# A four-layer graph network on one core: unread matmuls in TensorE's pauses, group 1's set-up products moved, and the last group's order rewritten

## The chip, the cores and the metric

One core of one Trainium2 chip runs the whole program as one launch. Its engines run side by side and wait for each other only through semaphores: TensorE (PE), VectorE (DVE), ScalarE (ACT), GpSimd (POOL) and SyncE (SP), which here only starts DMAs. The metric is the device time of one execution in microseconds (us).

## The reference, cut to what matters

A batch of 16 graphs, each of 512 nodes by 128 features, goes through four layers. Each is `x = layernorm(x + layer(x, adj))` over the features, in fp32.

```
x: (16, 512, 128), adj: (512, 512)
layer 0: concat([x, x*s, x*s*s, ...]) @ W + b      # s: sums over rows or columns of adj and of an adaptive softmax matrix
layer 1: batchnorm(relu(batchnorm((A_hat @ x) @ W1.T + b1)) @ W2.T + b2)   # statistics over all 16*512 rows
layer 2: twice relu(adj @ (h @ Wg + bg)); then for p = 1..4 an LSTM over windows of p nodes, whose last state
         replaces the last node of each window
layer 3: h = x @ fc.T + fcb; eight times h = h + 1/8 * (alph*0.5*(adj @ h - h) + h @ w_eff - h + x)
```

The eight Euler steps of layer 3 are linear in `h` and `x`. The kernel computes them as a polynomial in the matrix of the steps: x3 (the layer's input), two multiplications by powers of the matrix (`power1`, `power2`), combinations with precomputed coefficient matrices `e` (`coefs`), and two more multiplications by its cube, which a Horner scheme needs (`inner`, then `giant`). A constant row, `euler_bias`, stands for what `fcb` adds over the eight steps.

## The kernel before, in words

`D` is 128 features, `N` 512 nodes, in `NT` = 4 tiles of 128. A product that must be exact to fp32 is three matmuls of rounded parts (high x high, high x low, low x high; `matmul3`, lines 136 to 138), so an input of TensorE is first written as a high part (a cast, mostly on ACT) and a low part (the difference, on DVE or POOL). A PSUM bank holds 128 x 512 fp32.

The program has two halves.

The first half does layer 0 and layer 1 for all 16 batches. `phase_a` runs over slots q = 0..9 with a pair of batches in each: `products` (layer 0, ended on DVE), `aggregate` (A_hat times x, slot q-1, 24 matmuls of 128x512 for the pair) and `hidden` (times W1, slot q-2). Slot 0 has no aggregate yet and slot 8 no products. After it comes `second` (line 777), which waits for the batch norm over all rows and multiplies by W2 for each batch, each in two fp32 matmuls of 128x512. Then the block ends, with a barrier of all engines.

The second half works in groups of two batches, g = 0..7. The loop for group g does, on every engine, four things at once: the LSTMs of group g (layer 2) in eleven cells c0..c10; layer 3 of group g-1 (`L3_NAMES`); the `giant` products, their sum and the last norm of group g-2 (`DONE_NAMES`); the graph convolution of group g+1 (`FRONT_NAMES`). The order is written out by hand in tables, one list of names per engine and cell: an engine runs its part of cell c and then the names in list c. A cell's chain is: gate matmuls on TensorE, ACT (sigmoids and tanh), DVE (state), ACT, DVE (state and next input, high and low, `in_h`, `in_l`), and TensorE again. Between a cell's matmuls TensorE runs the names, and they are what fills the time the chain takes. For example, and only of TensorE:

```python
FILL_PE = [[], ["giant_2", "giant_3", "giant_0", "giant_1", "turn_0"], ["x3t_0", "power1a_0"],
           ["power1b_0", "power2_0", "gather0_0"], ["coefs0_0", "weight0_0"], ...
TAIL_PE = [["giant_2", "giant_3", "giant_0", "giant_1", "x3t_0", "x3t_1", "power1a_0", ...
LATE_PE, ... = ({1: ["lift_last", "bias"]}, ...      # added to FILL_PE's lists in group 1
```

Tables `START_*` and `ONCE_*` stand for the time before group 0 and for group 0; `FILL_*` with the `LATE_*` names for group 1; `FILL_*` for groups 2 to 6; `LAST_*` for group 7; `TAIL_*` has two lists behind it, layer 3 of group 7 with the `giant`s of group 6, and the `giant`s of group 7. What stands in the tail has no LSTM beside it.

Group 0 also computes constants of layer 3: the matrix powers, `lift` and `lift_last` (24 matmuls in all, the bias row's vectors lifted by the cube), `turn_vec`, `bias` (line 1921: the row times ones, into a bank, copied by DVE to `euler_bias`, semaphore `bias_kept`), and `split_e`, the low part of `e`.

`x3sum` takes the norm's statistics on DVE (line 1434); POOL turns them into mean and variance (lines 1179 to 1186) and into rstd and shift (line 1187, a power, and 1188), `root`; ACT applies them (line 1276), casts the high part (line 1313); POOL makes the low part (line 1206). `x3t` (line 1760) transposes the result; `power1a` and `power1b` are its product with the matrix, by halves of the tiles. `hturn` (line 1820) turns the LSTM's state back, `x3add` adds it to the layer's input.

## Time and profile before

| | us |
|---|---|
| median of 3 runs | 998.44 (998.06 to 1000.43) |
| the profiled execution, its own time | 999.66 |
| its span, first to last instruction | 997.7 |
| TensorE busy | 912.7 (91%) |
| VectorE busy | 648.7 (65%) |
| ScalarE busy | 578.3 (58%) |
| GpSimd busy | 309.7 (31%) |
| mean granted TensorE clock | 0.957 of full speed |

Busy times come from one profiled execution. A matmul's duration overlaps its neighbours' in the trace: what one costs in a dense stretch is the distance from its start to the next one's start. The granted clock has two levels, full speed (2.4 GHz) and half (1.2 GHz); a value between them for a stretch is a mean.

### The profile page before, as it was taken

Reading aid. Unit: us, or ns where it says so; the run is one execution under the profiler, and the core shown is the slowest. Engines: PE = TensorE matmul, PEld = TensorE weight load, DVE = VectorE, ACT = ScalarE, POOL = GpSimd, SP = SyncE. Lnnn points to the kernel's source line nnn. Section 1 sums busy time; section 2 is a strip of 40 time slices with the busy share of each in tenths; the row PEclk is TensorE's granted clock in tenths of the full one; section 3 lists DMA queues with packets and bytes.
Section 4 is the critical chain, followed back from the end, with each engine's and each line's share of the span. In section 5 each row is a group of like instructions: output and inputs, shape, how many; then the busy total and the mean of one; then the engine's idle time right before and its main releaser. Section 6 shows DMA issues by size and latency. Waiting matters only on the chain.

```text
span 997.7 us, 14843 instructions
## 1 busy us (share of the span) xinstructions
PE 912.7 (91%) x5034; PEld 790.2 (79%) x5034; DVE 648.7 (65%) x1554; ACT 578.3 (58%) x1292; POOL 309.7 (31%) x555
## 2 busy tenths in 40 slices
PE   6799996957999799999999999999999999999695
PEld 4688884446888479988998998898899899888584
DVE  6689994766577665576667667666666765755522
ACT  5366755742564457467657746755774684575331
POOL 3666551032210322144126215303521620230412
PEclk9799997978999989999999999999999999999897
DMA  5322101310100110101201010110110001001000
GB/s 174 117 75 64 68 28 42 148 55 9 32 1 12 42 33 11 43 1 43 64 1 43 28 38 11 33 64 1 43 64 1 12 22 33 1 11 33 1 22 22
DMA packets 26595, 38.55 MB, mean 39 GB/s; under 512 B 3333, under 2 KB 12422, under 8 KB 26010
## 3 DMA queue, kind: packets, MB, share of 16 engines
q1 hardware_dynamic: 26088, 36.05, 10.8%
q10 hardware_dynamic: 434, 1.57, 0.5%
q8 instruction: 40, 0.66, 0.3%
q14 instruction: 33, 0.27, 0.1%
HBM read 21.89 MB, written 15.73 MB: 38 GB/s over the span
## 4 chain that ended last, share of the span: by engine, by line
PE 57%; POOL 7%; DVE 7%; ACT 5%; issue 2%; ACTq 0%; DMA 0%; SPq 0%; POOLq 0%; DVEq 0%
PE psum L136 16%; PE psum L138 16%; PE psum L137 16%; PE psum L1707 2%; PE psum L1708 2%; PE psum L1711 2%; POOL x_rstd L1187 1%; ACT x L1276 1%; POOL out_rstd L1187 1%; ACT raw L1341 1%; POOL node_l L1197 1%; ACT gate L1245 1%; DVE x_stats L1434 1%; DVE nat_l L1579 1%; DVE tl L1482 1%
## 5 line engine op out<-in xcount | busy, mean ns | idle before, releaser
L1245 ACT ACTIVATE gate<-psum,gate_bias 128x256 f32<-128x256 f32 (+2 forms) x296 | 144.4, 559 | 88.0 <-PE psum L1711 70.2
L136 PE MATMUL psum<-in_h,wih_h 128*128 128x256 f32 (+2 forms) x312 | 108.0, 346 | 8.7 <-DVE in_l L1428 6.4
L137 PE MATMUL psum<-in_l,wih_h 128*128 128x256 f32 (+2 forms) x312 | 104.4, 335 | 0.0
L138 PE MATMUL psum<-in_h,wih_l 128*128 128x256 f32 (+2 forms) x312 | 104.3, 334 | 0.0
L1409 DVE TENSOR_TENSOR gate<-gate 128x256 f32<-128x256 f32 (+2 forms) x48 | 23.9, 499 | 93.3 <-ACT gate L1245 93.2
L1211 POOL TENSOR_TENSOR gate<-in_h,in_l 128x512 f32<-128x512 f32 x16 | 20.5, 1304 | 185.0 <-DVE in_l L1428 185.0
L136 PEld LDWEIGHTS psum<-in_h,wih_h 128*128 128x128 f32 x312 | 59.9, 192 | 20.5 <-DVE in_l L1428 9.9
L136 PE MATMUL psum<-e_h,th 128*128 128x384 f32 x180 | 62.6, 348 | 5.1 <-DVE tl L1482 3.3
L1248 ACT ACTIVATE gate<-cell 128x512 f32<-128x512 f32 (+2 forms) x80 | 40.2, 503 | 43.0 <-DVE cell L1412 35.2
L137 PEld LDWEIGHTS psum<-in_l,wih_h 128*128 128x128 f32 x312 | 60.0, 192 | 5.0 <-issue 0.2
L138 PEld LDWEIGHTS psum<-in_h,wih_l 128*128 128x128 f32 x312 | 60.0, 192 | 4.8
L138 PE MATMUL psum<-e_h,tl 128*128 128x384 f32 x180 | 61.5, 341 | 0.0
L137 PE MATMUL psum<-e_l,th 128*128 128x384 f32 x180 | 61.3, 341 | 0.0
L1707 PE MATMUL psum<-st_h,whh_h 128*128 128x256 f32 (+2 forms) x192 | 56.7, 313 | 0.4 <-DVE st_h L1417 0.4
L1708 PE MATMUL psum<-st_h,whh_l 128*128 128x256 f32 (+2 forms) x192 | 56.6, 312 | 0.0
L1206 POOL TENSOR_TENSOR x3l<-raw,x3h 128x512 fp32r<-128x512 f32 x15 | 19.4, 1297 | 119.1 <-ACT x3h L1313 119.1
L136 PE MATMUL psum<-adj_h,node_h 128*128 128x512 f32 x120 | 48.2, 401 | 5.1 <-POOL node_l L1197 5.1
L588 DVE SCALAR_TENSOR_TENSOR mix<-psum,coef,mix 128x256 f32<-128x256 f32 x96 | 46.3, 482 | 9.0 <-ACT mix L418 6.7
L1179 POOL TENSOR_TENSOR x_mv<-x_stats 128x4 f32<-128x4 f32 x32 | 10.6, 332 | 129.1 <-DVE x_stats L1434 129.1
L136 PE MATMUL psum<-pow_h,x3h 128*128 128x512 f32 x120 | 49.8, 415 | 0.0
L137 PE MATMUL psum<-pow_l,x3h 128*128 128x512 f32 x120 | 48.4, 403 | 0.0
L138 PE MATMUL psum<-pow_h,x3l 128*128 128x512 f32 x120 | 48.3, 402 | 0.0
(368 smaller groups left out, 2939.9 us busy)
## 6 DMA issues: line engine op xcount, KB each, us to landing
x_spill<-x SPq DMA_DIRECT2D x30, 256.0 KB, 2.0
xt<-in_x_t_dram SPq DMA_DIRECT2D x16, 256.0 KB, 2.7
raw<-x_spill SPq DMA_DIRECT2D x16, 256.0 KB, 2.9
o_spill<-xt SPq DMA_DIRECT2D x14, 256.0 KB, 2.0
xt<-o_spill SPq DMA_DIRECT2D x14, 256.0 KB, 3.2
x<-x_spill SPq DMA_DIRECT2D x14, 256.0 KB, 3.4
out_dram<-raw SPq DMA_DIRECT2D x14, 256.0 KB, 2.3
raw<-in_adj_t_dram ACTq DMA_DIRECT2D x1, 1024.0 KB, 8.9
```

Source lines behind the costliest of these rows:

```text
L136: pe.matmul(dst, lh, rh, start=start, stop=False, **kw)
L137: pe.matmul(dst, lh, rl, start=False, stop=False, **kw)
L138: return pe.matmul(dst, ll, rh, start=False, stop=stop, **kw)
L588: chain.link(nc.vector.scalar_tensor_tensor(out=m, in0=scaled_block(t, k), scalar=coef[:, k - 1, t:t + 1], in1=m, op0=ALU.mult, op1=ALU.add))
L1187: chain.link(nc.gpsimd.tensor_tensor(rstd, rstd, exponent[:, 0:rstd.shape[-1]], ALU.pow))
L1211: nc.gpsimd.tensor_tensor(gate[3 * j][:].rearrange("p (w c) -> p c w", c=4), f32(mod4(in2_h)[:, :, j, :]), f32(mod4(in2_l)[:, :, j, :]), A ...
L1245: nc.scalar.activation(gate[q][:, 0:n], banks[GATE_BANK[q]][:, 0:n], ACT.Tanh if q == 2 else ACT.Sigmoid, bias=gate_bias[:, p - 1, q:q + 1 ...
L1248: nc.scalar.activation(gate[2][:, 0:n], cell[:, 0:n], ACT.Tanh).then_inc(tanh_ready, 1)
L1409: nc.vector.tensor_tensor(gate[0][:, 0:n], gate[0][:, 0:n], gate[2][:, 0:n], ALU.mult)
L1707: pe.matmul(bank, tile(whh_h[:, p - 2, :], q), st_h[:, 0:n], start=False, stop=False)
L1708: pe.matmul(bank, tile(whh_l[:, p - 2, :], q), st_h[:, 0:n], start=False, stop=False)
L1711: pe.matmul(banks[GATE_BANK[q]][:, 0:n], tile(whh_h[:, p - 2, :], q), st_l[:, 0:n], start=False, stop=True).then_inc(gate_sum, 1)
```

## The change

Four things change.

In the first half TensorE gets `keep_busy`: matmuls of 128x512 into a bank that nothing reads, 79 of them at seven places, and 4 of 128x128 at the very start. They signal nothing. Two of the places bring waits of their own: one behind `weights_ready`, which the products waited for anyway, and one behind `bias_ready` in slot 0.

From group 0 to group 1, `hturn`, `x3add` and the first `x3sum` leave the end of group 0 and stand at the start of group 1 (`hlate`, `addlate`); group 0's state then has a place of its own, `whole_state`. `lift` goes to c1, `turn_vec` and `split_e` to c2, `lift_last` to c3, `bias` to c4, before `coefs0_0`. `power1a_0` waits for `v5_kept` and no longer for `bias_kept`; `coefs0` waits for `bias_kept`. The load of the layer's input (`x3load`) waits for an earlier event.

In group 7, `power1a_0` stands in c3 instead of c2, half of `power2_1` in c6 instead of c7, the first products of layer 3 use banks 2 and 3 instead of those that `giant` uses, and `x3add` and `x3sum` go batch by batch between the low parts of `inner`. The moments of the norm and the low part of x3 are computed on DVE (`spread_of`, `x3low`), and POOL keeps the power and one product (`power_of`).

In the tail, `power1_0` stands before `x3t_1`. The last group's `inner_0` runs the first three of its four contraction parts before it waits for the last `gl`, and the `giant`s are split by contraction: `gianta` does tiles m = 0, 1, which need the first batch-half of the inner result, `giantb` does m = 2, 3. The last half of the output is scaled by ACT for one batch and by DVE for the other.

```diff
+            def keep_busy(times, bank):
+                operand = wmix_h[:].rearrange("p k d -> p (k d)")
+                for _ in range(times):
+                    pe.matmul(banks[bank][:], wmix_h[:, 0, :], operand[:, 0:N], start=True, stop=True)
...
             pe.wait_ge(weights_ready, 1)
+            keep_busy(4, 0)
...
+                if q == PAIRED:
+                    keep_busy(9, 4)
                 if now:
                     products(q, 3)
                 if q == 0:
+                    keep_busy(12, 7)
                     pe.wait_ge(dinv_spread, 1)
...
+                    pe.wait_ge(bias_ready, 1)
+                    keep_busy(8, 6)
+                if q == 1:
+                    keep_busy(12, 6)
                 if one:
...
             phase_a(slot)
+            keep_busy(18, 4)
...
                 second(2 * i + 1, 1)
+            keep_busy(16, 4)
...
         def product_banks(g, j):
-            return banks[0:2] if at_end(g, j) else UB
+            if isinstance(g, int) and g == G - 1:
+                return banks[0:2] if j == 1 else banks[2:4]
+            return UB
...
+        TAIL_PE = [["gianta_0", "gianta_1", "giantb_1", "giantb_0", "x3t_0", "power1a_0", "power1b_0", "x3t_1", "power2_0",
+                    "power1a_1", "power1b_1", "power2_1", "coefs0_0", "coefs1_0", "coefs0_1", "coefs1_1", "inner_0", "inner_1"],
+                   ["gianta_0", "gianta_1", "giantb_1", "giantb_0"]]
...
+            def spread_of(norm, tiles, asked, first=0):
+                for i, ap in enumerate(tiles, first):
+                    ins = nc.vector.bn_stats(norm.stats[:, i, :], ap)
+                chain.link(ins)
...
+                nc.vector.tensor_tensor(norm.rstd[:, columns], gap, var, ALU.add).then_inc(asked, 1)
...
+            def x3low(g, j):
+                n = GB * g + j
+                dve.wait_ge(x3_hi, n + 1)
+                high, low = x3_parts(g, j)
+                nc.vector.tensor_tensor(low[:], x3[:, j, :, :], f32(high[:]), ALU.subtract).then_inc(x3_lo, 1)
...
+            def giant_first(g, half):
+                pe.wait_ge(inner_lo, 2 * g + 1)
+                if half == 1:
+                    pe.wait_ge(inner_summed, 2 * (g + 1))
+                for t in (2 * half, 2 * half + 1):
+                    by_cube(t, vh, vl, range(0, 2), True)
+            def giant_rest(g, half):
+                pe.wait_ge(inner_lo, 2 * (g + 1))
+                for t in (2 * half, 2 * half + 1):
+                    mm = by_cube(t, vh, vl, range(2, NT), True)
+                mm.then_inc(giant_done, 1)
...
             def lift_last():
-                pe.wait_ge(x3_summed, GB)
+                pe.wait_ge(power_lo[0], 2)
...
             def bias():
                 pe.wait_ge(vt_kept, 2)
+                pe.wait_ge(power_lo[0], BABY)
```

TensorE's order in slots 0 and 1 of the first half: what is new stands with +, what was there is the row with - and its renumbered twin. `L701` (of the changed kernel) is `keep_busy`, `L765`/`L778` the four matmuls that wait for `dinv`.

```order
 L138 MATMUL psum<-wmix_h,xtl 128x256
-L765 MATMUL psum<-z,ones 128x128 [waits dinv_spread]
-L765 MATMUL psum<-z,ones 128x128 x3
+L701 MATMUL psum<-wmix_h 128x512 x12
+L778 MATMUL psum<-z,ones 128x128 [waits dinv_spread]
+L778 MATMUL psum<-z,ones 128x128 x3
+L701 MATMUL psum<-wmix_h 128x512 [waits bias_ready]
+L701 MATMUL psum<-wmix_h 128x512 x7
 L136 MATMUL psum<-wmix_h,xth 128x384 [waits mixed,xt_lo,xt_hi]
```

Twelve unread matmuls stand ahead of the wait for `dinv_spread`, and eight, with a wait for `bias_ready`, between it and slot 1's products; twelve more stand ahead of slot 1's aggregate.

TensorE's order in group 1, from the end of c1's names to the first power, before (`L1921` is `bias`, `L1760` is `x3t_0`):

```order
L138 MATMUL psum<-pow_h,vpad_l 9x512
L1921 MATMUL psum<-raw 128x128 [waits vt_kept]
L1921 MATMUL psum<-raw 128x128 x3
L136 MATMUL psum<-in_h,wih_h 128x512 [waits gate_on,state_ready]
...
L138 MATMUL psum<-in_h,wih_l 128x512
L1760 MATMUL psum<-ident,raw 128x128 [waits vt_kept,x3_ready]
L1760 MATMUL psum<-ident,raw 128x128 x3
L136 MATMUL psum<-pow_h,x3h 128x512 [waits bias_kept,x3_lo]
```

and now (`L2013` is `turn_vec`, `L1841` is `x3t_0`):

```order
L138 MATMUL psum<-in_h,wih_l 128x512
L2013 MATMUL psum<-ident,raw 128x9 [waits bc_kept,vt_kept]
L2013 MATMUL psum<-ident,raw 128x9 x3
L1841 MATMUL psum<-ident,raw 128x128 [waits vt_kept,x3_ready]
L1841 MATMUL psum<-ident,raw 128x128 x3
L136 MATMUL psum<-pow_h,x3h 128x512 [waits v5_kept,x3_lo]
```

`bias` with its wait for `vt_kept` no longer stands ahead of c2's gate matmuls, and `turn_vec` stands behind them.

TensorE's order in the tail, from the last `giant` matmul of group 6 on, before (`L1760` is `x3t`, first of batch 0, then of batch 1):

```order
L138 MATMUL psum<-th,pow_l 128x256
L1760 MATMUL psum<-ident,raw 128x128 [waits y_summed,x3_ready]
L1760 MATMUL psum<-ident,raw 128x128 x3
L1760 MATMUL psum<-ident,raw 128x128 [waits x3_ready]
L1760 MATMUL psum<-ident,raw 128x128 x3
L136 MATMUL psum<-pow_h,x3h 128x512 [waits x3_lo]
```

and now (`L1841` is `x3t_0`; `x3t_1` is the second pair of it, behind `power1_0`):

```order
L138 MATMUL psum<-th,pow_l 128x256
L1841 MATMUL psum<-ident,raw 128x128 [waits x3_ready]
L1841 MATMUL psum<-ident,raw 128x128 x3
L136 MATMUL psum<-pow_h,x3h 128x512 [waits x3_lo]
...
L138 MATMUL psum<-pow_h,x3l 128x512
L1841 MATMUL psum<-ident,raw 128x128 [waits x3_ready]
L1841 MATMUL psum<-ident,raw 128x128 x3
L136 MATMUL psum<-pow_h,x3h 128x512 [waits power_lo0,x3_lo]
```

The wait for `y_summed` is gone from `x3t_0`, and all twelve matmuls of batch 0's first power stand ahead of batch 1's transposes.

## Rows read from the trace of the kernel before

**Rows 1.** The page, engines: busy time, share of the span, instructions.

```profile
PE 912.7 (91%) x5034; PEld 790.2 (79%) x5034; DVE 648.7 (65%) x1554; ACT 578.3 (58%) x1292; POOL 309.7 (31%) x555
```

**Rows 2.** Windows: us; busy (instructions) per engine; granted TensorE clock; DMA.

```profile
347.50:355.60 8.10, 8.04 (x24) 6.65 (x25) 3.03 (x8) 3.19 (x7) 3.19 (x11) 0.50 0.01 2
938.00:950.00 12.00, 5.80 (x19) 4.62 (x20) 2.56 (x9) 3.87 (x8) 8.13 (x21) 0.57 0.00 0
950.00:980.00 30.00, 27.12 (x158) 25.03 (x156) 9.04 (x24) 10.14 (x30) 0.57 (x2) 1.00 0.06 18
```

**Rows 3.** Timeline of PE: start, duration, engine, line, operation [idle before <-releaser].

```profile
29.75 0.66 PE L136 MATMUL psum<-wmix_h,xth 128*128 128x384 f32 x1 [2.65 <-issue]
...
44.14 0.51 PE L136 MATMUL psum<-ahat_h,x1h 128*128 128x512 f32 x1 [3.75 <-POOL x1l L314]
...
46.17 0.63 PE L136 MATMUL psum<-ahat_h,x1h 128*128 128x512 f32 x1
...
46.59 0.63 PE L137 MATMUL psum<-ahat_l,x1h 128*128 128x512 f32 x1
...
48.59 0.40 PE L136 MATMUL psum<-ahat_h,x1h 128*128 128x512 f32 x1
...
51.41 0.34 PE L136 MATMUL psum<-wmix_h,xth 128*128 128x384 f32 x1
```

**Rows 4.** Timeline of DVE and ACT before the first aggregation.

```profile
33.37 0.16 DVE L613 SCALAR_TENSOR_TENSOR shift<-mv,rstd 128x8 f32<-128x8 f32 x1
...
35.81 0.47 ACT L418 ACTIVATE mix<-psum,coef 128x256 f32<-128x256 f32 x1 [2.01 <-PE psum L138]
```

**Rows 5.** Timeline of PE and POOL, last slots of the first half's main phase.

```profile
153.60 0.50 PE L136 MATMUL psum<-ahat_h,x1h 128*128 128x512 f32 x1 [3.02 <-POOL x1l L314]
...
155.44 1.29 POOL L314 TENSOR_TENSOR x1l<-x,x1h 128x512 fp32r<-128x512 f32 x1 [1.90 <-ACT x1h L437]
...
158.04 0.40 PE L136 MATMUL psum<-ahat_h,x1h 128*128 128x512 f32 x1
```

**Rows 6.** Timeline of PE and DVE where the second phase begins.

```profile
169.18 5.49 PE L777 MATMUL psum<-adjn,w 128*128 128x512 f32 x6 [5.09 <-ACT adjn L511]
...
175.66 0.69 DVE L678 COPY xt<-psum 128x512 f32<-128x512 f32 x1 [1.36 <-PE psum L777]
```

**Rows 7.** Timeline of PE in group 1, steps c1 to c4.

```profile
347.56 2.07 PE L1921 MATMUL psum<-raw 9*128 9x128 f32 x8 [6.11 <-DVE raw L1665]
...
361.84 0.40 PE L136 MATMUL psum<-pow_h,x3h 128*128 128x512 f32 x1
...
372.22 0.41 PE L136 MATMUL psum<-e_h,th 128*128 128x384 f32 x1 [1.81 <-DVE e_l L1645]
```

**Rows 8.** Timeline of PE, last group, step c4.

```profile
881.00 0.44 PE L136 MATMUL psum<-in_h,wih_h 128*128 128x340 f32 x1 [2.11 <-DVE in_l L1428]
```

**Rows 9.** Timeline of all engines, from the last group's end to the program's end.

```profile
925.64 2.56 POOL L1211 TENSOR_TENSOR gate<-in_h,in_l 128x512 f32<-128x512 f32 x2 [29.07 <-DVE in_l L1428]
...
926.90 1.84 DVE L1501 TENSOR_TENSOR tl<-raw,th 128x512 fp32r<-128x512 f32 x1 [0.74 <-ACT th L1337]
...
932.96 0.21 POOL L1179 TENSOR_TENSOR x_mv<-x_stats 128x4 f32<-128x4 f32 x1 [4.76 <-DVE x_stats L1434]
...
936.23 1.65 ACT L1276 ACTIVATE raw<-raw,x_shift,x_rstd 128x128 f32<-128x128 f32 x4 [6.18 <-POOL x_shift L1188]
...
944.78 1.11 PE L1760 MATMUL psum<-ident,raw 128*128 128x128 f32 x4 [6.20 <-ACT raw L1276]
...
958.50 0.34 PE L136 MATMUL psum<-e_h,th 128*128 128x384 f32 x1
...
972.30 0.39 PE L136 MATMUL psum<-gh,pow_h 128*128 128x256 f32 x1 [1.04 <-DVE gl L1491]
...
980.45 0.58 PE L136 MATMUL psum<-th,pow_h 128*128 128x256 f32 x1 [2.28 <-DVE tl L1501]
...
987.81 0.69 DVE L1507 TENSOR_TENSOR raw<-raw,psum 128x512 f32<-128x512 f32 x1 [1.14 <-PE psum L138]
```

More of the change, by code:

```diff
@@ L696, in _ @@
         def _(pe):
+            def keep_busy(times, bank):
+                operand = wmix_h[:].rearrange("p k d -> p (k d)")
+                for _ in range(times):
+                    pe.matmul(banks[bank][:], wmix_h[:, 0, :], operand[:, 0:N], start=True, stop=True)
+            pe.wait_ge(ones_ready, 1)
+            for _ in range(4):
+                pe.matmul(tile(banks[0][:], 0), ones[:], ones[:], start=True, stop=True)
             pe.wait_ge(c_nv, 32)
@@ L862, in at_start, with whole_state @@
             return isinstance(n, int) and n < GB
+        def whole_state(g, j):
+            return whole[:, (NT * GB + j * NT) * D:(NT * GB + (j + 1) * NT) * D] if g == 0 else gate[3 * j][:]
         def at_end(g, j):
@@ L1040, in second_half @@
-        TAIL_PE = [["giant_2", "giant_3", "giant_0", "giant_1", "x3t_0", "x3t_1", "power1a_0", "power1b_0", "power1a_1", "power1b_1",
-                    "power2_0", "power2_1", "coefs0_0", "coefs1_0", "coefs0_1", "coefs1_1", "inner_0", "inner_1"],
-                   ["giant_2", "giant_3", "giant_0", "giant_1"]]
-        TAIL_ACT = [["x3norm_0", "x3split_0", "x3norm_1", "x3split_1", "x3t_0", "x3t_1", "out_0", "power1_0", "power1_1", "out_1",
-                     "power2_0", "power2_1", "coefs0_0", "coefs1_0", "coefs0_1", "coefs1_1", "inner_0", "inner_1"],
+        DONE_NAMES = ("giant", "gianta", "giantb", "ysum", "outsum", "out", "outhalf")
@@ new lines, in second_half @@
+        LAST_POOL = FILL_POOL[:10] + [["whole", "x3early_0", "x3early_1"]]
+        TAIL_PE = [["gianta_0", "gianta_1", "giantb_1", "giantb_0", "x3t_0", "power1a_0", "power1b_0", "x3t_1", "power2_0",
+                    "power1a_1", "power1b_1", "power2_1", "coefs0_0", "coefs1_0", "coefs0_1", "coefs1_1", "inner_0", "inner_1"],
+                   ["gianta_0", "gianta_1", "giantb_1", "giantb_0"]]
+        TAIL_ACT = [["x3norm_0", "x3split_0", "x3norm_1", "x3split_1", "x3t_0", "power1_0", "x3t_1", "out_0", "power2_0", "out_1",
+                     "power1_1", "power2_1", "coefs0_0", "coefs1_0", "coefs0_1", "coefs1_1", "inner_0", "inner_1"],
@@ L1106, in step, with run @@
                     piece(name)
-        def run(cell_step, pieces, start, once, fill, last, tail, late={}):
+        def run(cell_step, pieces, start, once, following, fill, last, tail):
             step(-1, None, pieces, [start], lstm=False, l3=False, done=False)
             step(0, cell_step, pieces, once, l3=False, done=False)
-            step(1, cell_step, pieces, [names + late.get(c, []) for c, names in enumerate(fill)], done=False)
+            step(1, cell_step, pieces, following, done=False)
             for g in range(2, G - 1):
@@ L1351, in out_half @@
                 act.wait_ge(out_shift, g + (2 - half))
-                for j in range(GB):
+                for j in range(GB if half == 1 else 1):
                     for t in (2 * half, 2 * half + 1):
@@ L1790, in coefs, with by_cube @@
                     mm.then_inc(coef_done, 1)
-            def by_cube(t, high, low):
-                for m in range(NT):
+            def by_cube(t, high, low, parts=range(NT), shared=False):
+                for m in parts:
                     mm = matmul3(pe, UB[t // 2][:, (t % 2) * GB * D:(t % 2 + 1) * GB * D],
```

151 lines of the change are left out of this document (100 added, 51 removed), and 1 row of the table ONCE_DVE.

## The prediction, made before the changed kernel ran

> **What bounds the kernel now.** I read the page's list of engines first. TensorE is busy 912.7 us of 997.7, the next engine 648.7 [rows 1], so the time is TensorE's: its busy time plus 85 us in which it waits. A gain can come from three places: a wait that goes, a stretch in which the same matmuls run at half clock, and what stands behind the last matmul. Then I read the windows around its pauses for the granted clock, and the timeline for each pause, its releaser and the engine behind that.
>
> The windows show what a pause costs beyond itself. From 347.5 to 355.6, right behind a pause of 6.11 us, the granted clock is 0.50, so half (1.2 GHz), with TensorE busy 8.04 of 8.10; from 938 to 950 it is 0.57; in the dense stretch from 950 to 980 it is 1.00 [rows 2, 7]. The same 128x512 matmul follows its predecessor after 0.42 us at half (46.17 to 46.59) and after 0.235 at full speed (12 of them from 48.59 to 51.41 take 2.82) [rows 3]. So each 128x512 matmul at half costs 0.19 more.
>
> The trace has two kinds of pause here. Those of the first half and of the tail have no other matmul that could run; those in groups 2 to 6 are not touched.
>
> **Part A, unread matmuls in the first half.** None is waited for, so one costs only what it pushes back.
>
> - Start: 4 stand between the logits and the first products, which nothing else fills. At half they are 4 x 0.42 = 1.7, lost if all of it is pushed; if the products behind them get full speed sooner, 3 of these at 0.19 apiece come back (0.5) beyond the 1.7. I take a loss of 0.3, near the good end, since TensorE has work before and behind; the bounds are 1.7 lost and 0.5 gained.
> - Slots 0 and 1: the products of slot 1 start at 29.75 after 2.65 idle, and at a longer spacing than those at 51.41 [rows 3]: I read half clock. Eight unread ones stand in that pause (8 x 0.235 = 1.9), and their wait for `bias_ready` holds nothing, since POOL waits for the same event before its first bias addition, long before. DVE has the shift of the norm at 33.37 + 0.16 = 33.5, but ACT's queue holds a scaling that waits for TensorE until 35.81, and the norm's application stands behind it [rows 4]. Products at full speed end that wait up to 2.6 earlier, and with it the chain ACT, POOL (low part), first aggregate. The aggregate starts at 44.14 after 3.75 idle, with its first 10 matmuls near half clock, and its 24 end at 51.41 [rows 3]. After: 12 unread ones (12 x 0.235 = 2.8) fit in the 3.75; the aggregate starts at 42.7 to 43 and its 24 take 5.64: end 48.6. Gain 2.8.
> - Slot 8: an aggregate starts at 153.60 after 3.02 idle, its second batch at 158.04; POOL's low part for that one ends at 155.44 + 1.29 = 156.73 [rows 5]. Twelve matmuls at full speed would end at 156.4, so POOL decides: 158.04 - 156.8 = 1.2.
> - Before `second`: idle 5.09, then fp32 matmuls at half until DVE's copy of the second batch's bank at 175.66 [rows 6]. The first six take 5.49, 0.86 a piece or more, where full speed gives half. 18 unread ones are 18 x 0.235 = 4.2, inside 5.09. The copy comes 2.8 earlier.
> - Behind `second`: 16 x 0.235 = 3.8 end at about the barrier; 0.3 lost, 0.3 gained from turns at full speed. Nothing.
>
> Sum A: -0.3 + 2.8 + 1.2 + 2.8 = 6.5. Bounds: 4 if the fills at half clock push what follows twice, 8 if the start gains.
>
> The pauses of 3.02, 3.75 and 5.09 in the rows above all have slow matmuls behind them [rows 3, 5, 6], the dense stretch has none [rows 2]. The Trainium skill ("TensorE: Matmul & The Clock Gate", Part 1, The HAM clock gate) says that the half clock is the default state and that activity releases it; by that rule matmuls that nobody reads hold the clock as well as others. The trace agrees on the pauses, and no row of it shows an unread matmul, which is what rival 1 rests on.
>
> **Part B, group 1.** `bias` starts at 347.56, after 6.11 of idle that DVE's sum for `lift_last` ended, and stands ahead of c2's gates; `power1b` starts at 361.84, `coefs0_0` at 372.22 after 1.81 more of idle, behind the low part of `e` [rows 7]. Now c2's gates need only their own chain. `lift` (3.3 us with its second product, of the size of `lift_last` at 12 x 0.235 = 2.8 and a little) and `turn_vec` (1.0) leave the path before c0, so the chain of c0 and c1 starts about 4 earlier, and `power1a_0` starts 3.8 to 4.8 earlier. c3's names then start at 357.4 to 359.2 instead of 361.84, but `lift_last` stands there too, 2.8. So c4 gains 0.7 at least (361.84 - 358.3 - 2.8), and what the idle of 1.81 and the half clock behind it give. A pause of about 5.8 remains in c1 to c2, and the new wait of `coefs0_0` for `bias_kept` has DVE's state of c4 queued ahead of it: it can be as long as the old one, 1.81. The bounds are 0 (the moved wait only takes another's place) and 4.5 (0.7 + 1.81 + 2.0 of half clock). I take 2.0, the middle: `bias` ends a wait of the same length, but the low part of `e`, which held the step, is two cells earlier. The load moved on SP waits for an earlier event, and nothing is queued behind it there: no cost.
>
> **Part C1, group 7 with its own order.** c4's gates start at 881.00 after 2.11 idle [rows 8], and behind them runs half clock. `power1a_0` in c3, 6 matmuls of 0.235 = 1.4, fills that pause. `coefs0_0` then starts 1.5 earlier and c5 2.1 earlier. But the half of `power2_1` in c6 waits for DVE's low part, which holds c7 near its old place. I take 1.3 of the 2.1 at the end of c10; bounds 0 and 2.5.
>
> **Part C2, the tail.** All starts here are 1.3 earlier. The `giant`s of group 6 no longer wait for the second low part and end at 934.0. Batch 0 of x3: before, DVE's statistics, then POOL's chain from 932.96 to ACT's application at 936.23 [rows 9], 3.3 us. After: seven small DVE instructions of 0.16 (the kind of the shift in rows 4), 1.1 us, and POOL's power and product, 1.35; and they start before the second low part. The shift is ready at about 932, x3 is applied, and `x3t_0` and `power1_0` start right behind the `giant`s, at 934.0 and 935.0. Batch 1 follows during `power1_0` and `power2_0`. The 48 power matmuls run dense at 0.235: 11.3 us, plus 0.9 and 0.8 for the turns, so `coefs0_0` starts at 934.0 + 13.0 = 947.0. Before, it started at 958.50, behind 6.20 idle and a stretch at 0.57 clock [rows 2, 9]. That is 11.4 (1.3 of them C1's).
>
> `coefs` is as long as before. `inner_0` waited 1.04 for the last low part (972.30); three quarters of its contraction now stand ahead of that wait: 1.2. The last `giant`s start at 980.45, after 2.28 idle, and run at half for about 3 us (0.58 for the first of 128x256, against 0.39 at 972.30); TensorE ends as DVE adds the last half, 987.81 [rows 9]. Split by contraction, the first halves run in the idle time: 2.28 + 1.4 (24 matmuls of 128x256 at half instead of full, 3 us of it, half is excess) + 0.7 from the order = 4.4 with the clock held. So the last `giant` ends 17.0 earlier. Behind it stood 997.7 - 987.8 = 9.9: moments on DVE instead of POOL save 0.8, two applications on ACT instead of four 0.8, less one more wait 0.5: 1.1.
>
> C2 without C1's 1.3: 17.0 + 1.1 - 1.3 = 16.8. Bounds: 12, if batch 1 is late for its powers and half clock stays, and 18.
>
> A row speaks for another cost here. DVE's low part at 926.90 took 1.84 us, beside POOL's sum of two inputs from 925.64 to 928.20 [rows 9]; the same instruction elsewhere takes 0.69. The Trainium skill ("SBUF — State Buffer", "Who interferes with whom") says that a DVE instruction with two SBUF inputs and a GpSimd one that reads SBUF block each other for a whole instruction. The trace agrees here. By that rule `x3low` and the moments can each be held by POOL's power (1.04 us): two such stalls cost 2.1 on DVE, which the dense stretch of powers hides in my sum and rival 2 does not.
>
> **The sum.** 6.5 + 2.0 + 1.3 + 16.8 = 26.6. Against the profiled execution's own time: 999.66 - 26.6 = 973.1. That execution is 1.2 above the median of the three, so the median to expect is 971.9; I say 972.0.
>
> **The rivals.**
>
> 1. *The unread matmuls do not hold the clock.* They run at half themselves, 12 x 0.42 = 5.0 instead of 2.8, overrun the pauses of 3.0 to 5.1 and delay what follows. For it: where long pauses were, the clock needed some us of dense matmuls before it rose (44.14 to about 48.3). Against it: they start while it is still at full speed. A then gives 1 instead of 6.5: 977.5.
> 2. *The tail becomes DVE's.* DVE does low part, additions, moments of two batches and the low parts of the transposes in one queue, with the stalls above. If batch 1's x3 comes 3 later than its powers, TensorE idles 3 and the clock may fall (12 matmuls x 0.19 = 2.3). C2 gives 12 instead of 16.8: 976.8.
> 3. *Group 1 gains nothing*, since a new wait takes the place of the old: 974. Its opposite, group 1 at 4.5 and the start at its best, gives 968.
> 4. *Slower.* TensorE's granted clock falls to half in group 1 and in the tail and stays there, since every new order has shorter but more pauses. From 934 to 971 some 35 us of matmuls at full speed would take 70; the gain is gone when 27 us or more of full-speed work runs at half in addition, and the time is about 972 + 35 = 1007. Against it: the dense stretch at 1.00 from 950 to 980 has pauses of 1 to 2.3 in or behind it [rows 2, 9]. It decides only if 27 us of matmul work is hit.
>
> **Chances.** Forecast, 969.5 to 974.5: 0.47. Rival 1: 0.15. Rival 2: 0.17. Rival 3: 0.07, its opposite 0.08. Several small failures at once, 979 to 995: 0.04. Rival 4: 0.02. The range from 966 to 980 leaves out some 0.1 to 0.2. A measurement of this kernel tells about 0.3% (3 us) from no change: faster 0.97, same 0.01, slower 0.02.
>
> **What would show it.** Right: PEclk 1.00 around 44, 154 and 170 us, with line 136's first aggregate at about 43; `second`'s first copy at full cadence; `bias` behind c4 and no 6-us pause with half clock behind it before c2's gates; in the tail no idle above 1 us between the `giant`s of group 6 and `coefs0_0`, which starts at about 947 less A and B, so near 938.5; the last `giant`s with clock 1.00. Wrong: fills whose spacing is 0.42; `x3t_1` or the second batch's first power waiting for DVE's `x3low`; an idle time before `coefs0_0` in group 1 as long as before; and a whole time above 980 or below 966.

## The result, and the profile after

The changed kernel takes 984.97 us (median of 4, 984.0 to 986.26) against 999.23 for the kernel before: a ratio of 0.9858, 95% interval 0.9839 to 0.9877. That is 14.3 us less, or about half of the 26.6 that the prediction summed up, and 5 us above its range. Two single executions far outside all others, 2249.22 us of the kernel before and 1497.9 us of giants_whole, are left out of every figure in this document.

The two profiled executions have own times of 999.66 and 986.26 and spans of 997.7 and 984.1, 13.6 apart. This is the page of the changed kernel, its list of engines (against [rows 1]) and the granted clock in 40 slices:

```profile
PE 922.5 (94%) x5121; PEld 798.1 (81%) x5121; DVE 652.3 (66%) x1586; ACT 577.3 (59%) x1290; POOL 303.8 (31%) x521
PEclk9999999988899889999999999999999999988999
```

TensorE is busy 9.8 us more, and the span is 13.6 shorter: 23.4 us of idle time are gone. Much of that idle time is now filled with work that nobody reads: the 79 unread matmuls are some 18.6 us of the busy time, an estimate from the spacing of 0.235 in [rows 3]. What is left in the clock's row stands in slices of groups 0 and 1, and in two near the end, where group 7 is.

I cut both traces at five events that both have. The span of each piece, and how long the clock was at half in it (twice one minus the granted clock of the window, times its length; the first window starts at 5 us). The clock is given with two decimals, so such a time is good to about 2 us in the first half and in groups 0 and 1, and to 0.8 in group 7:

| piece | before, us (at half) | after, us (at half) | gain | predicted |
|---|---|---|---|---|
| to the first transposes of the second half | 205.20 (24.0) | 199.99 (3.9) | 5.2 | 6.5 |
| groups 0 and 1, to the gates of c5 | 173.08 (38.1) | 176.65 (38.9) | -3.6 | 2.0 |
| groups 2 to 6, to the first `inner` of the last full step | 469.55 (0.0) | 469.57 (0.0) | 0.0 | 0 |
| group 7, to its `hturn` | 79.61 (3.2) | 83.92 (10.1) | -4.3 | 1.3 |
| tail, to the last matmul | 60.06 (13.2) | 44.98 (0.0) | 15.1 | 15.7 |
| behind the last matmul | 10.2 | 9.0 | 1.2 | 1.1 |

The predicted 16.8 for the tail are divided here at the last matmul. The first half and the tail came out at 21.5 of 23.3. Groups 0 and 1 and group 7 were to give 3.3 and cost 7.9: 11.2 of the 13 us that are missing.

The windows that answer to [rows 2], then two of the first half, all of the changed kernel (columns as there):

```profile
347.50:355.60 8.10, 8.10 (x28) 6.43 (x28) 2.14 (x5) 2.81 (x6) 4.05 (x11) 0.74 0.35 98
938.00:950.00 12.00, 10.99 (x52) 8.74 (x51) 6.22 (x16) 8.13 (x19) 5.26 (x12) 1.00 0.07 22
950.00:980.00 30.00, 25.38 (x175) 24.89 (x174) 12.65 (x46) 7.31 (x24) 2.10 (x3) 1.00 0.03 10
...
36.00:44.00 8.00, 6.99 (x33) 6.67 (x33) 5.46 (x15) 7.11 (x17) 6.96 (x7) 0.79 0.41 131
44.00:52.00 8.00, 8.00 (x39) 6.74 (x38) 5.51 (x17) 1.35 (x3) 7.26 (x8) 1.00 0.62 230
```

In the tail the stretch that was at 0.57 with 5.80 of 12 us busy is now at 1.00 with 10.99 busy. The aggregate of slot 0 now runs at 1.00. Group 1 still has half clock.

Group 1's rows, against [rows 7], from the timelines of DVE and PE (start, duration; in brackets the idle time ahead and what ended it):

```profile
344.91 0.69 DVE L1466 TENSOR_TENSOR st_l<-gate,st_h 128x512 fp32r<-128x512 f32 x1
345.52 0.16 DVE L1737 COPY vpad<-psum 128x12 f32<-128x12 f32 x1
...
345.93 0.20 DVE L1739 TENSOR_TENSOR vpad_l<-vpad,vpad_h 128x36 fp32r<-128x36 f32 x1
```

```profile
331.62 1.09 PE L1801 MATMUL psum<-ident,xt 128*128 128x128 f32 x4 [2.98 <-DVE raw L1593]
...
346.27 0.77 PE L136 MATMUL psum<-pow_h,x3h 128*128 128x512 f32 x1 [5.70 <-DVE vpad_l L1739]
...
355.72 0.40 PE L136 MATMUL psum<-pow_h,x3h 128*128 128x512 f32 x1
...
362.83 0.39 PE L136 MATMUL psum<-pow_h,vpad_h 128*9 128x512 f32 x1 [2.75 <-DVE tl L1545]
...
373.43 0.41 PE L136 MATMUL psum<-e_h,th 128*128 128x384 f32 x1 [0.90 <-DVE euler_bias L1748]
```

The pause of 6.11 ahead of `bias` is gone, and others took its place: 5.70 ahead of `power1a_0`, 2.75 ahead of `lift_last`, 0.90 ahead of `coefs0_0`. The 5.70 is the one that I had priced at nothing. `power1a_0` writes the bank that `turn_vec`'s result lies in, so it waits for `v5_kept`; DVE's three copies of that result take 0.16 to 0.20 each, but they stand in DVE's queue behind c2's cell, which ends with `st_l` at 345.60. A pause of 2.98 stands further ahead, at group 1's `turn_0`, which waits for DVE's additions of the state (`addlate`, L1593); the kernel before had 0.34 there. It is in every profile with the new order of group 1, and no run takes it out. With the first half's 5.2 us taken off, `power1b_0` (355.72) starts 0.9 earlier than before and `coefs0_0` 6.4 later.

Group 7's two pauses, from PE's timeline (against [rows 8]):

```profile
878.06 0.43 PE L136 MATMUL psum<-in_h,wih_h 128*128 128x340 f32 x1 [0.70 <-DVE in_l L1475]
...
881.60 0.69 PE L136 MATMUL psum<-e_h,th 128*128 128x384 f32 x1 [1.86 <-DVE tl L1545]
...
904.05 0.47 PE L136 MATMUL psum<-pow_h,x3h 128*128 128x512 f32 x1 [2.50 <-DVE tl L1540]
```

The pause of 2.11 ahead of c4's gates shrank to 0.70, as forecast, and came back one step on: `coefs0_0` now waits 1.86 for the low part of the second power. The half of `power2_1` in c6 waits 2.50 for a low part that DVE writes behind c6's cell, and c7's gates stand behind it in TensorE's queue.

The tail, against [rows 9]:

```profile
930.95 0.65 PE L1926 MATMUL psum<-ident,gate 128*128 128x128 f32 x4 [0.21 <-POOL gate L1258]
...
935.08 0.39 PE L136 MATMUL psum<-th,pow_h 128*128 128x256 f32 x1 [0.52 <-DVE tl L1566]
...
939.29 0.50 PE L136 MATMUL psum<-pow_h,x3h 128*128 128x512 f32 x1 [0.71 <-DVE x3l L1578]
...
942.21 0.60 PE L1841 MATMUL psum<-ident,raw 128*128 128x128 f32 x4
...
951.42 0.34 PE L136 MATMUL psum<-e_h,th 128*128 128x384 f32 x1
...
964.02 0.28 PE L136 MATMUL psum<-gh,pow_h 128*128 128x256 f32 x1
...
969.62 0.28 PE L136 MATMUL psum<-th,pow_h 128*128 128x256 f32 x1
```

No pause above 0.71 stands between the `giant`s of group 6 and `coefs0_0`, where there were 6.20 and 1.19. Counted from `hturn` (927.44 before, 930.13 after), `coefs0_0` starts 9.8 earlier (10.1 forecast), `inner_0` another 1.2 (1.2), the last matmul another 4.1 (4.4).

### The profile page after: what moved, and what is told of

Read it like the earlier page. It is cut to its first block, busy times and chain, and to the rows that moved or that the text cites. A ratio compares the mean times of both kernels' runs of the same rounds, so it can differ in the third digit from the quotient of the medians.

```text
span 984.1 us, 15023 instructions
## 1 busy us (share of the span) xinstructions
PE 922.5 (94%) x5121; PEld 798.1 (81%) x5121; DVE 652.3 (66%) x1586; ACT 577.3 (59%) x1290; POOL 303.8 (31%) x521
## 4 chain that ended last, share of the span: by engine, by line
PE 55%; DVE 9%; POOL 7%; ACT 5%; issue 2%; ACTq 0%; POOLq 0%; DVEq 0%
PE psum L136 16%; PE psum L138 15%; PE psum L137 15%; PE psum L1787 2%; PE psum L1788 2%; PE psum L1791 2%; POOL out_rstd L1224 1%; POOL x_rstd L1224 1%; ACT x L1323 1%; ACT raw L1388 1%; ACT gate L1292 1%; DVE tl L1545 1%; POOL node_l L1242 1%; DVE x_stats L1481 1%; DVE nat_l L1659 1%
## 5 line engine op out<-in xcount | busy, mean ns | idle before, releaser
L1258 POOL TENSOR_TENSOR gate<-in_h,in_l 128x512 f32<-128x512 f32 x14 | 17.9, 1307 | 167.4 <-DVE in_l L1475 167.4
L138 PE MATMUL psum<-adj_h,node_l 128*128 128x512 f32 x120 | 48.4, 403 | 0.0
```

Source lines behind the costliest of these rows:

```text
L138: return pe.matmul(dst, ll, rh, start=False, stop=stop, **kw)
```

## The experiments

Their medians, each against the kernel before on the same chip, and the pieces of the profiled execution as above. The groups of runs were on different chips, on which the kernel before took 998.7 to 1000.4, so a difference between medians of two groups can be off by some 1 us. The last three rows are single executions, without a ratio:

| kernel | median us | ratio, 95% interval | first | groups 0, 1 (at half) | group 7 (at half) | tail |
|---|---|---|---|---|---|---|
| the changed kernel | 984.97 | 0.9858, 0.9839 to 0.9877 | 199.99 | 176.65 (38.9) | 83.92 (10.1) | 44.98 |
| group7_old | 981.47 | 0.9813, 0.9776 to 0.985 | 199.51 | 177.62 (39.1) | 79.63 (3.2) | 45.07 |
| group1_old | 977.81 | 0.9779, 0.9754 to 0.9805 | 200.27 | 172.20 (34.4) | 79.87 (0.0) | 45.12 |
| both_old | 975.46 | 0.9757, 0.973 to 0.9784 | 199.86 | 170.57 (34.1) | 79.67 (3.2) | 45.10 |
| no_fills | 993.04 | 0.9928, 0.9904 to 0.9952 | 206.65 | 175.87 (38.7) | 81.35 (3.3) | 44.98 |
| fills_only | 992.57 | 0.9931, 0.9905 to 0.9956 | 200.59 | 171.57 (34.3) | 79.63 (3.2) | 60.14 |
| turnvec_c1 | 981.87 | 0.9826, 0.9795 to 0.9856 | 201.05 | 171.50 (34.3) | 79.86 (0.0) | 45.02 |
| turnvec_gather | 977.27 | 0.9779, 0.9741 to 0.9816 | 200.21 | 169.78 (30.6) | 81.23 (3.2) | 45.08 |
| power1a_c2 | 983.03 | 0.9836, 0.9802 to 0.9869 | 199.40 | 176.57 (35.3) | 80.71 (3.2) | 45.14 |
| power2_c7 | 987.51 | 0.9883, 0.9853 to 0.9913 | 199.92 | 179.18 (43.0) | 81.95 (6.6) | 45.16 |
| giants_whole | 993.92 | 0.9955, 0.9933 to 0.9977 | 200.28 | 178.10 (39.2) | 81.16 (3.2) | 52.06 |
| pool_moments | 989.98 | 0.9907, 0.9891 to 0.9924 | 200.62 | 178.26 (39.2) | 81.23 (3.2) | 48.32 |
| best_a | 972.44 | 0.9754, 0.9718 to 0.979 | 200.75 | 166.85 (23.4) | 78.07 (0.0) | 45.05 |
| after_b | 984.23 | | 200.68 | 174.32 (31.4) | 83.75 (10.1) | 45.06 |
| after_c | 983.63 | | 200.50 | 177.69 (39.1) | 79.89 (0.0) | 44.98 |
| best_b | 971.14 | | 200.60 | 166.97 (23.4) | 78.08 (0.0) | 45.08 |

**Both losing orders put back: group7_old, both_old, group1_old.**

```diff
# group7_old
-        LAST_PE = ... [["x3t_0"], ["power1a_0", "power1b_0", "power2_0"], ...
+        LAST_PE = ... [["x3t_0", "power1a_0"], ["power1b_0", "power2_0"], ...
-                  ["x3t_1", "power1a_1", "power1b_1", "power2a_1"], ["power2b_1"], ...
+                  ["x3t_1", "power1a_1", "power1b_1"], ["power2a_1", "power2b_1"], ...
# group1_old: ONCE_* as before, and for group 1
+        NEXT_PE, NEXT_ACT, NEXT_DVE, NEXT_POOL = FILL_* with the LATE_* names of the kernel before
#   and the waits, banks and the place of group 0's state as before; both_old is the two together
```

> The changed kernel with group 7's matmul order as before: power1a_0 back in c2, both halves of power2_1 in c7. Theory: in the trace of the changed kernel the same matmuls stand 2.9 us later (against the kernel before) at c7's gates than at c4's, 3.3 us behind a pause of 2.50 before the first half of power2_1 in c6 and 2.0 us behind half clock in c4 to c5; so this order is what lost 4.3 us in group 7, and putting it back gives 980.5 to 982 (3 to 4.5 less than the changed kernel's 984.97). Rival: group 7 lost its time through the new banks or through x3add and x3sum batch by batch, and this kernel stays at 985 within 1.

> The changed kernel with group 7's matmul order as before and with group 1 wholly as before (hturn, x3add and the first x3sum at the end of group 0, lift, turn_vec, lift_last and bias at their old places, power1a_0 waiting for bias_kept). Theory: both moves lose, group 1 by 3.6 to 4.3 and group 7 by 3 to 4.5, so 976 to 978.5. Rival: the loss of group 1 is only paid forward by something both orders share (the end of group 0), and this kernel is no faster than the one with group 7's order alone, 981.

> The changed kernel with group 1 alone as before. Theory: 980.7 to 981.4 (3.6 to 4.3 less than 984.97), with power1a_0 no longer waiting 5.70 us for the low part that turn_vec writes, and bias again behind 6 us of idle with half clock after it. Rival: group 1's loss depends on what follows it (its state enters group 2 at the same distance), and the time stays within 1 us of 985.

Measured 981.47, 975.46 and 977.81. Group 7's order costs 3.5 or 2.4 us of the median, by what it stands beside, and group 1's 7.2 or 6.0, more than the trace's 3.6 had made me expect. One reason shows in the table: behind the unread matmuls, groups 0 and 1 in their old order take 170.57 to 172.20 and no longer the 173.08 of before. The loss is therefore larger than the difference to the kernel before. both_old came out a little below its range and group1_old 3 us below its own. For group 1 no rival held: nine profiles have the changed kernel's instructions there and took 174.32 to 179.18, four have the old order and took 170.57 to 173.08. For group 7 the medians alone do not decide it, since the intervals of the changed kernel and group7_old overlap, as do those of group1_old and both_old; the pieces of the traces, compared at equal half clock below, do.

**The unread matmuls: no_fills, fills_only.**

```diff
# no_fills: out of the changed kernel; fills_only: into the kernel before
-            keep_busy(4, 0)
-                if q == PAIRED:
-                    keep_busy(9, 4)
-                    keep_busy(12, 7)
-                    pe.wait_ge(bias_ready, 1)
-                    keep_busy(8, 6)
...
```

> The changed kernel without any unread matmul and without the wait for bias_ready. Theory: they give 5.5 to 6.5 in the first half, and this kernel takes 990.5 to 991.5. Rival: the start's four cost what they give elsewhere and the real gain is under 4: 988 or less. A second rival, that the clock they hold also helps the second half, gives 993 or more.

> The kernel before with the unread matmuls of the first half alone (and their wait for bias_ready). Theory: they take 5.2 to 6.6 us off the first half wherever the second half stands, and what the clock does later averages out: 992.5 to 994.5. Rival: the second half's clock follows from when it starts, and the kernel before lost by chance in group 1, so that 990.5 or less comes out; the other rival, that only the whole change makes them pay, gives 996 or more.

Measured 993.04 and 992.57: without them the changed kernel is 8.1 slower (its profiled execution was its fastest, so its trace shows less), and alone they make the kernel before 6.1 faster (from 998.71 on that chip). At the end of the first half the traces are 6.7 and 4.6 apart. The term of 6.5 was right in kind and size. The second rival of no_fills, that they help the second half too, is at its bound of 993 and not refuted; groups 0 and 1 of no_fills do not support it (175.87 against 176.65), those of fills_only, 1.5 shorter than in the kernel before, do a little.

**What in group 1: turnvec_c1, turnvec_gather.**

```diff
# turnvec_c1 (the same move in NEXT_DVE)
-        NEXT_PE = [["hlate"], ["turn_0", "lift"], ["turn_vec", "x3t_0", "power1a_0"], ...
+        NEXT_PE = [["hlate"], ["turn_0", "lift", "turn_vec"], ["x3t_0", "power1a_0"], ...
# turnvec_gather: beside it
-                   ["power1b_0", "power2_0", "lift_last", "gather0_0"],
+                   ["power1b_0", "power2_0", "gather0_0", "lift_last"],
```

> The changed kernel with turn_vec one cell earlier, in c1 behind lift, on TensorE and on DVE. Theory: in the changed kernel power1a_0 waited 5.70 us, not for a product but for the bank that turn_vec's DVE copies free, and these stood behind c2's cell in DVE's queue; here the copies stand ahead of that cell, power1a_0 starts near 342 instead of 346.3 with no pause above 2 us before it, and the time is 980.5 to 982.5, so 2.5 to 4.5 of group 1's 6 to 7 come back. Rival: c3 is bound by DVE's state of c2 and by the second wait, of lift_last (2.75), and the time stays at 984 or more.

> As the one before, and gather0_0 ahead of lift_last in c3 on TensorE and DVE. Theory: lift_last waited 2.75 us for DVE's low part of the first power, which stands behind c3's cell; the 12 matmuls of gather0_0 (2.8 us) need nothing from there and fill it. 978 to 980, 2 to 3 less than with turn_vec alone, and within 2 us of the kernel with the old group 1 (977.81). Rival: bias and coefs0_0 then wait for DVE's sum of lift_last, the pause only moves to coefs0_0, and the gain over turn_vec alone is under 1.

Measured 981.87, inside its theory, and 977.27, a little below its own. PE's pauses in steps c2 to c4 of group 1 of turnvec_c1:

```profile
338.08 1.05 PE L2013 MATMUL psum<-ident,raw 9*128 9x9 f32 x8 [0.77 <-DVE raw L1732]
...
357.28 0.59 PE L136 MATMUL psum<-pow_h,vpad_h 128*9 128x512 f32 x1 [2.80 <-DVE tl L1545]
...
369.34 0.41 PE L136 MATMUL psum<-e_h,th 128*128 128x384 f32 x1 [0.90 <-DVE euler_bias L1748]
```

The 5.70 is 0.77, and the piece of groups 0 and 1 is 171.50, no longer than with the old order. A part of these 5.2 us can be the clock, since this profiled execution is its kernel's fastest and has 34.3 us at half against 38.9. But after_b, the changed kernel with only 31.4 at half, took 174.32, still 2.8 more. The 2.80 ahead of `lift_last` stays, and with `gather0_0` ahead of it the piece is 169.78. So the wait for the bank was the larger part of group 1's loss, and the wait of `lift_last` the next. How much the latter is stays rough: the two traces differ by 1.7, of which the clock can be most (30.6 us at half against 34.3), and the medians by 4.6.

**What in group 7: power1a_c2, power2_c7.** Each puts back one of the two moves of group7_old.

> The changed kernel with group 7's power1a_0 back in c2, the split of power2_1 kept. Theory: of group 7's 3.5 us this is 1.5 to 2: the matmuls in c3 let c4 start earlier but made coefs0_0 wait for DVE's low part (1.86) with half clock in c4 and c5. 983 to 983.5. Rival: it alone decides, 981.5.

> The changed kernel with group 7's power2_1 whole in c7, power1a_0 kept in c3. Theory: the half in c6 waited 2.50 us for DVE's low part ahead of c7's gates, which were ready before (1.82 idle then), and half clock came behind; back in c7 it gives 2 to 3: 982 to 983. Rival: it only fills the pause that c7's gates have anyway, 984.5 to 985.5.

Measured 983.03 and 987.51. The first is as forecast; the second contradicts both its theory and its rival. The table says why neither median can be read for group 7. power2_c7 took 179.18 us in groups 0 and 1, where its instructions are those of the changed kernel, with 43.0 us at half clock; in group 7 it was 2.0 shorter, with 3.5 us less at half. power1a_c2 was 3.2 shorter there, with 6.9 us less at half. With the price of one us at half that the next experiment gives (0.4), the order's own share is 0.6 for the one move and 0.4 for the other; that is 1.0 together, short of the 1.6 found below for both, so neither share is exact. By the medians alone I would have concluded that power2_1 in c6 did good.

**The same program again: after_b, after_c, best_b** (no edit).

> The changed kernel itself, a second profile. Theory: group 7's segment was 83.92 us in the first profile with 10.1 us at half clock, and 81.2 in two others of the same order with 3.2 us at half: the clock of one execution decides some 2.7 us, and the same program shows another amount of half clock here, with segment lengths that follow it at about 0.4 us per us. Rival: the half clock follows from the program's own timing, and this profile repeats 84 within 0.3.

> The changed kernel itself, a third profile. Both theories as for the second profile.

> The kernel with turn_vec in c1, gather0_0 first and group 7's old order, a second profile. Theory: groups 0 and 1 took 166.85 us with 23.4 us at half clock in its first profile; at the 30 to 34 us that its nearest relatives had it would be 170 to 171.5, so between 971 and 976. Rival: its order avoids the half clock, and 166.9 within 0.5 comes again.

Own times were 984.23, 983.63 and 971.14. Two windows of group 7 in each profile of the changed kernel, first the profile shown above, then after_b, then after_c:

```profile
878.00:890.00 12.00, 10.08 (x43) 9.80 (x44) 4.24 (x11) 8.63 (x23) 2.81 (x11) 0.72 0.07 23
...
902.00:910.00 8.00, 5.95 (x26) 5.24 (x27) 3.06 (x8) 2.62 (x7) 0.00 (x0) 0.79 0.00 0
```

```profile
878.00:890.00 12.00, 10.44 (x47) 10.44 (x48) 4.23 (x10) 7.67 (x22) 1.15 (x2) 0.72 0.07 23
...
902.00:910.00 8.00, 8.00 (x43) 7.25 (x44) 2.65 (x6) 4.21 (x10) 0.00 (x0) 0.79 0.00 0
```

```profile
878.00:890.00 12.00, 9.42 (x55) 8.66 (x55) 5.51 (x13) 8.89 (x24) 4.05 (x12) 1.00 0.08 23
...
902.00:910.00 8.00, 7.17 (x46) 6.47 (x47) 3.44 (x7) 4.75 (x12) 0.00 (x0) 1.00 0.06 18
```

And the pauses there in after_c, from PE's timeline:

```profile
882.92 0.44 PE L136 MATMUL psum<-e_h,th 128*128 128x384 f32 x1 [1.89 <-DVE tl L1545]
...
902.68 0.47 PE L136 MATMUL psum<-pow_h,x3h 128*128 128x512 f32 x1 [2.50 <-DVE tl L1540]
```

The pauses are the same, 1.86 and 1.89, 2.50 and 2.50. The clock fell behind them twice and did not the third time. Group 7's piece was 83.92 and 83.75 with 10.1 us at half clock, and 79.89 with none. So one us at half costs this piece about 0.4. after_b alone repeated the first profile, as the rival had it; after_c brought what the theory had said of one program. At the same 3.2 us at half, the new order takes 81.16 to 81.35 (no_fills, turnvec_gather, giants_whole, pool_moments) and the old one 79.61 to 79.67 (before, group7_old, both_old, fills_only). That is 1.6 for the order, and 1.8 between the orders without any half clock there (79.86 to 79.89 in turnvec_c1, group1_old and after_c, 78.07 and 78.08 in best_a and best_b); the other 2.7 of the 4.3 go with the clock of these executions. best_b came to 166.97 with 23.4 us at half, as its rival had it. That the order avoids the half clock is not shown by it: turnvec_gather has the same instructions in groups 0 and 1, and took 169.78 with 30.6 at half.

**The parts of the tail: giants_whole, pool_moments.**

```diff
# giants_whole
-        TAIL_PE = [["gianta_0", "gianta_1", "giantb_1", "giantb_0", "x3t_0", ...
+        TAIL_PE = [["giant_2", "giant_3", "giant_0", "giant_1", "x3t_0", ...      # inner_0 whole as well
# pool_moments
-                (power_of if g == G - 1 else root)(x3_norm[j], ...)
+                root(x3_norm[j], ...)                                             # the same for out_norm, and on DVE
-        TAIL_POOL = [["outsum"], ...
+        TAIL_POOL = [["x3split_0", "x3split_1", "outsum"], ...                    # x3low off DVE's list
```

> The changed kernel with the contraction splits undone: the giants of groups 6 and 7 and the last inner_0 whole, each behind its full wait, as before. Theory: in the prediction these splits were 4.4 at the last giants and 1.2 at inner_0; the tail of 44.98 us (from hturn to the last matmul) becomes 49.5 to 51, and the time 989 to 991. Rival: with the clock at full speed in the tail most of the 4.4 was half clock that does not come back, and it is 2 to 3: 987 to 988.

> The changed kernel with the moments of the last norms and the low parts of x3 back on POOL. Theory: each batch's x3 then comes 2 later from the moments (1.9 on POOL against 0.9) and the low part (1.28 against 0.69), which the giants of group 6 hide for batch 0 only in part, and the end loses 1: 987.5 to 990, with a pause of 2 to 3 ahead of the first powers. Rival: DVE was the crowded engine there, POOL takes the work beside it and only the end loses: 985 to 986.

Of giants_whole the profiled execution took 991.01 and the median is 993.92, above its theory: three executions lie at 991 to 992 with a granted clock of 0.974 to 0.976, three at 996 to 997 with 0.965. Where the slower three lost their 5 us is not known, since none of them was profiled. I read the one trace: the tail is 7.1 longer, above the theory's 4.5 to 6, and what stands behind it 1.1 shorter, so 6.0 in all. Its pauses, from PE's timeline, at the `giant`s of group 6, at `inner_0` and at the last `giant`s:

```profile
933.78 0.58 PE L136 MATMUL psum<-th,pow_h 128*128 128x256 f32 x1 [3.47 <-DVE tl L1566]
...
967.17 0.36 PE L136 MATMUL psum<-gh,pow_h 128*128 128x256 f32 x1 [1.14 <-DVE gl L1556]
...
975.29 0.39 PE L136 MATMUL psum<-th,pow_h 128*128 128x256 f32 x1 [2.28 <-DVE tl L1566]
```

The last one is the 2.28 of [rows 9] again, and without half clock behind it. What was not in my sum is the 3.47: with the moments on DVE, its queue is longer than before, and whole `giant`s wait for all of it (that pause was 1.91 in the kernel before).

pool_moments came to 989.98, the upper end of its theory: 3.3 in the tail and 1.8 behind it. Its pauses ahead of `x3t_0` and of the first power:

```profile
938.19 0.66 PE L1841 MATMUL psum<-ident,raw 128*128 128x128 f32 x4 [1.55 <-ACT raw L1323]
...
940.89 0.63 PE L136 MATMUL psum<-pow_h,x3h 128*128 128x512 f32 x1 [2.04 <-POOL x3l L1251]
```

**The repaired kernel: best_a.** turnvec_gather with group 7's order as before.

> The changed kernel with turn_vec in c1, gather0_0 ahead of lift_last, and group 7's matmul order as before. Theory: both repairs add: 9.8 less than the changed kernel by segments of the traces (groups 0 and 1 at 169.8 to 171.5, group 7 at 79.6), so 974 to 976, equal to the kernel with both old orders (975.46) within 1.5. Rival: the group 7 segment depends on where the clock falls and not on the order, and this kernel stays at 977.3, where the one with the new group 7 was.

Measured 972.44, ratio 0.9754 (0.9718 to 0.979): 12.5 less than the changed kernel, and below what I expected. It is not told apart from both_old (975.46) by their intervals. Its pieces are 166.85 and 78.07, with less half clock in the two together than in any other kernel. That it lies at the prediction's 972.0 is chance: its groups 0 and 1 gave 6.2 where 2.0 were forecast, its first half 4.5 where 6.5 were, and in group 7 it has the old order. From its page, to be read against the one of the changed kernel above:

```profile
PE 913.8 (94%) x5121; PEld 791.3 (82%) x5121; DVE 652.4 (67%) x1586; ACT 576.9 (60%) x1290; POOL 304.2 (31%) x521
PEclk9999999978999999999999999999999999999998
```

The same 5121 instructions of TensorE are busy 8.7 us less, which the time at half clock explains; the other 6.4 of the 15.1 between the two spans are idle time.

## Why the prediction was wrong

Step by step, as the prediction put it:

- **First half, 6.5.** By the medians right (6.1 alone, 8.1 within the change). In the trace it is 5.2. The start lost nothing; 0.8 of the difference is the first load, which landed later (first matmul at 3.76, not 2.94; 2.96 and 3.36 in no_fills and both_old). Slots 0 and 1 gave 1.7 and not 2.8: the products did run at full speed until they waited 2.60 for DVE's mixing at 37.01, and then ran at half for some 3 us (0.79 from 36 to 44). Slot 8 gave 1.2 of 1.2, `second` 2.6 of 2.8.
- **Group 1, 2.0. This step failed.** The sentence was "`power1a_0` starts 3.8 to 4.8 earlier". It started 8.0 earlier by the trace's time, but 5.2 of these are the first half's, so 2.8, behind a pause of 5.70; and `power1b_0`, which was to start 2.6 to 4.4 earlier, started 0.9 earlier. I had written down the new wait (`v5_kept` for `bias_kept`) and priced only the wait that it replaced. I did not ask where DVE's copies stand: behind c2's cell. Nor did I price the wait of `lift_last` for the first power, 2.75, though it was in the diff. Of the pause of about 5.8 that I had left in c1 to c2, 2.98 stood there, ahead of `turn_0`. And I took 0 as the lower bound, with the reason that a moved wait only takes another's place. It can also be longer: the piece cost 3.6 against before in this profile (1.2 in after_b, 4.6 in after_c), and 6 to 7 by the medians against the same kernel with the old order.
- **Group 7, 1.3. This step failed too.** The sentence was that `power2_1`'s half "holds c7 near its old place". The wait for DVE's low part (2.50) stands ahead of c7's gates, which had waited only 1.82 there, and 6 matmuls stand behind the wait and ahead of the gates. And the pause that `power1a_0` filled came back at `coefs0_0` (1.86), since ACT's casts for the second power stood behind a scaling that waits for POOL. The order costs 1.6, the clock of this execution 2.7 more, which is bad luck and no fault of the reasoning.
- **Tail, 16.8.** It gave 16.3, and each term in it held: 9.8 of 10.1, 1.2 of 1.2, 4.1 of 4.4, 1.2 of 1.1. The rival of a tail bound by DVE did not come. DVE's low part beside POOL's sum was slow again, 1.83 at 929.60 against 1.84 in [rows 9]. The stalls of 1.04 that I had feared for DVE beside POOL's power fell on the other engine, as the next rows show, in which DVE starts first each time.

From the timelines of DVE and POOL in the changed kernel:

```profile
934.34 0.69 DVE L1566 TENSOR_TENSOR tl<-raw,th 128x512 fp32r<-128x512 f32 x1
...
938.55 0.69 DVE L1578 TENSOR_TENSOR x3l<-raw,x3h 128x512 fp32r<-128x512 f32 x1 [0.54 <-ACT x3h L1360]
```

```profile
934.50 1.40 POOL L1232 TENSOR_TENSOR x_rstd<-x_rstd,exponent 128x4 f32<-128x4 f32 x1 [3.61 <-DVE x_rstd L1498]
...
937.50 1.01 POOL L1232 TENSOR_TENSOR x_rstd<-x_rstd,exponent 128x4 f32<-128x4 f32 x1 [1.31 <-DVE x_rstd L1498]
938.58 0.72 POOL L1233 TENSOR_TENSOR x_shift<-x_mv,x_rstd 128x4 f32<-128x4 f32 x1
```

DVE keeps its 0.69. POOL's power takes 1.40 beside it, and 1.01 at 937.50, where DVE runs an addition of which one input lies in PSUM; its small product takes 0.72 behind `x3low` where the one at 935.98 took 0.20. The Trainium skill ("SBUF — State Buffer", "Who interferes with whom") says that a DVE instruction with two SBUF inputs and a GpSimd one that reads SBUF exclude each other and that issue order decides who waits. The trace agrees.

- **The cases.** What happened lay in "several small failures at once, 979 to 995", with a chance of 0.04. The bounds of groups 1 and 7 stopped at 0, so with the first half and the tail as forecast, as they nearly came, nothing above 972.0 + 2.0 + 1.3 = 975.3 was left. Had they reached as far below nothing as above it (-4.5 and -2.5), the upper end would have been 973.1 + 6.5 + 3.8 = 983.4 from these two terms alone, for the profiled execution, which took 986.26. The listed cases outside 966 to 980 also add up to 0.06 only, where the prediction speaks of 0.1 to 0.2.

What stays open: why the clock falls behind a pause of 1.9 or 2.5 us in one execution and not in another. The runs show only that the same program has both.

## What to carry to other kernels

When a wait is exchanged for another, find the instruction that signals the new one and read what stands ahead of it in its own engine's queue; that, and not its duration, is the price, and several such waits can cost more than the one that went. A dependence through a bank counts like one through data.

Work put into a pause helps only if nothing that it needs comes later than the pause ends, and if what stands next in the queue has no wait of its own: here the pause only moved on to `coefs0_0`.

With a clock that falls behind short pauses in some executions, compare kernels piece by piece, with the time at half clock beside each piece. A median of four that differs by 2 or 3 us says little about the piece that was edited.

## What the runs showed of the hardware

- Unread 128x512 matmuls hold TensorE's granted clock at full speed over pauses of 3 to 5 us: 24.0 us at half in the first half became 3.9 or 0.0, in every kernel that had them, and stayed at 24.2 in no_fills.
- Behind the pause of 6.11 (before) and that of 5.70 (the changed kernel) in group 1 the clock was at half. Behind group 7's pauses of 1.9 and 2.5 us it was at half in two of three profiles of one program, and at full speed in the third.
- One us at half clock cost about 0.4 us in group 7 ((83.92 - 79.89) / 10.1). By the spacings of [rows 3] a dense stretch loses 0.44 of it ((0.42 - 0.235) / 0.42).
- A DVE instruction with two SBUF inputs took 1.83 us where POOL's sum had started first and 0.69 otherwise; with DVE first, POOL's power took 1.40 instead of 1.01.
